# Where the rope scores of a step are issued in a decoder layer: behind product 7 of the step ahead

## The reference

```python
c_q = h @ w_q_down                       # 384 wide, h is the layer norm of x
c_kv = h @ w_kv_down                     # 128 wide, the latent keys and values
q_lat = einsum('bhsd,hdr->bhsr', q_nope(c_q), wuk)           # 32 heads
scores = einsum('bhsr,btr->bhst', q_lat, c_kv)               # latent scores
       + einsum('bhsd,btd->bhst', rope(q_rope(c_q)), k_rope) # rope scores
probs = softmax(mask(scores / sqrt(192)))
out = einsum('bhst,btr->bhsr', probs, c_kv)                  # "values" below
x = x + (out @ wuv per head) @ w_out
```

## Time and profile before

| what | value |
|---|---|
| median of 3 runs | 1907.11 us (1906.49 to 1908.13) |
| profiled execution, its own time | 1908.23 us |
| span in that profile | 1906.4 us |
| PE busy | 1896.1 us, 99% of the span |
| DVE busy | 1548.0 us, 81% |
| ACT busy | 1184.1 us, 62% |
| POOL busy | 1039.9 us, 55% |
| granted TensorE clock | full in every slice |
| chain that ended last | PE 94%, DMA 2%, DVE 2%, POOL 1% |

### The profile page before, as it was taken

One profiled execution on the slowest core, in us unless ns is written; L12 is line 12 of the kernel. 1 busy time (PEld: TensorE's weight loads), 2 busy tenths in 40 slices (PEclk: granted clock), 3 DMA queues, 4 the chain that ended last, 5 costly groups with the idle time before them and its releaser, 6 DMA issues.

```text
span 1906.4 us, 32258 instructions
## 1 busy us (share of the span) xinstructions
PE 1896.1 (99%) x9920; PEld 1595.8 (84%) x9920; DVE 1548.0 (81%) x3168; ACT 1184.1 (62%) x2904; POOL 1039.9 (55%) x1019
## 2 busy tenths in 40 slices
PE   9999999999999999999999999999999999999999
PEld 7888888888888888888888888888888877888887
DVE  6778888888888888888888787887888889996677
ACT  5457767675858575766556555565666668766441
POOL 5458777787869696965555656555665411000000
PEclk9999999999999999999999999999999999999999
DMA  9839575657475665699747375474738386557645
GB/s 362 332 109 318 136 257 136 249 129 260 134 261 145 227 180 192 206 327 314 190 148 230 77 231 149 152 219 124 231 94 276 113 284 233 206 213 258 222 150 176
DMA packets 328154, 393.27 MB, mean 206 GB/s; under 512 B 271616, under 2 KB 272384, under 8 KB 313088
## 3 DMA queue, kind: packets, MB, share of 16 engines
q1 hardware_dynamic: 328064, 392.21, 63.3%
HBM read 236.46 MB, written 155.71 MB: 206 GB/s over the span
## 4 chain that ended last, share of the span: by engine, by line
PE 94%; DMA 2%; DVE 2%; POOL 1%; issue 0%; SPq 0%; ACT 0%; DVEq 0%; POOLq 0%; ACTq 0%
PE at_out L1325 11%; PE at_out L1329 10%; PE at_out L1326 10%; PE at_qbank L55 7%; PE at_qbank L57 7%; PE at_qbank L56 7%; PE at_qbank L1649 3%; PE at_score L1286 3%; PE at_score L1289 2%; PE at_score L1649 2%; PE at_out L1649 2%; PE at_turned L1300 2%; PE at_value L55 2%; PE at_value L56 2%; PE at_value L57 2%; PE at_qbank L1652 2%
## 5 line engine op out<-in xcount | busy, mean ns | idle before, releaser
L2686 DVE TENSOR_TENSOR at_acc<-at_out,at_acc 128x512 f32<-128x512 f32 x640 | 438.5, 688 | 127.6 <-PE at_out L1329 120.4
L2315 POOL TENSOR_TENSOR at_acc<-at_stage,at_acc 128x512 f32<-128x512 f32 x256 | 331.8, 1296 | 174.4 <-ACT at_stage L1791 164.8
L1325 PE MATMUL at_out<-at_wvo,at_val_hi 128*128 128x512 f32 x896 | 365.6, 408 | 2.1 <-DVE at_acc L2686 1.2
L1329 PE MATMUL at_out<-at_wvo,at_val_lo 128*128 128x512 f32 x896 | 351.3, 392 | 0.0
L1326 PE MATMUL at_out<-at_wvo,at_val_hi 128*128 128x512 f32 x896 | 349.9, 391 | 0.0
L1791 ACT ACTIVATE at_stage<-at_out 128x512 f32<-128x512 f32 x256 | 153.0, 599 | 94.1 <-PE at_out L1329 82.0
L1329 PEld LDWEIGHTS at_out<-at_wvo,at_val_lo 128*128 128x128 f32 x896 | 168.1, 188 | 38.8
L1325 PEld LDWEIGHTS at_out<-at_wvo,at_val_hi 128*128 128x128 f32 x896 | 168.7, 188 | 32.6 <-DVE at_acc L2686 6.3
L1326 PEld LDWEIGHTS at_out<-at_wvo,at_val_hi 128*128 128x128 f32 x896 | 169.1, 189 | 25.5
L1832 ACT ACTIVATE at_pT<-at_turned 128x256 fp32r<-128x256 f32 x128 | 49.0, 383 | 227.3 <-PE at_turned L1300 226.4
L1827 ACT ACTIVATE at_probs<-at_probs,at_row_stats 128x128 f32<-128x128 f32 (+1 forms) x512 | 184.1, 361 | 8.9 <-DVE at_row_stats L2633 8.9
(11 more groups left out here) (323 smaller groups left out, 5042.3 us busy)
## 6 DMA issues: line engine op xcount, KB each, us to landing
parts_d<-at_rope_tmp SPq DMA_DIRECT2D x32, 1024.0 KB, 7.1
at_qrope<-parts_d SPq DMA_DIRECT2D x128, 256.0 KB, 4.5
wvo_d<-at_wvo SPq DMA_DIRECT2D x16, 2048.0 KB, 7.6
at_wvo<-wvo_d SPq DMA_DIRECT2D x16, 2048.0 KB, 8.5
ff_w_d<-ff_w SPq DMA_DIRECT2D x21, 1024.0 KB, 6.4
ff_w<-ff_w_d SPq DMA_DIRECT2D x21, 1024.0 KB, 4.8
ab_raw<-in_w_heads SPq DMA_DIRECT2D x32, 576.0 KB, 6.4
wvo_d<-at_wvo SPq DMA_DIRECT2D x16, 1024.0 KB, 9.8
```

The costliest lines, as they stand in the source:

```text
L1325: pe.matmul(out, hi, weight[:, 0], start=start, stop=False, skip_group_check=True)
L1329: pe.matmul(out, lo, weight[:, 0], start=False, stop=True, skip_group_check=True).then_inc(out_ready, 1)
L2315: pool.tensor_tensor(at, stage[group][z][:], at, ALU.add).then_inc(pool_added, 1)
L2686: dve.tensor_tensor(at, outb[FACTORS[name][2]][:], at, ALU.add).then_inc(added, 1)
```

## The change

The four rope-score matmuls of a step leave their place at the head of the step two ahead, and are issued half a step sooner: step s now issues those of step s+3, right behind product 7. Of the first steps, those of step 2 go to the end of `opening`, which is the same place in the order; those of step 4 stay at the head of step 2 of pass 0; step 1 of pass 0 issues none. In the second half of the last pass, where product 7 comes ahead of product 5, they come behind a half of a transposition for cross-attention and ahead of product 5. Nothing is computed otherwise, and no other engine's program changes.

```diff
                 absorb_head(0, first + 8, first + 7)
-
-            def next_scores(m, s, end, kind, first):
+                score_ropes(0, 2, 0)
+
+            def ropes_sooner(m, s, end, kind):
+
+                t = s + 3
+                if t < end and not opens(m, s, 1):
+                    score_ropes(m, t, group_of(kind, t))
+
+            def next_rests(m, s, end, kind, first):
                 use, t = USE[kind], s + 2
-                if t < end:
-                    score_ropes(m, t, group_of(kind, t))
-                if s + 1 < end:
-                    turn(m, s + 1)
                 if t < end:
                     score_rests(m, t, first - AFTER[kind] if t < 4 else first + use[2 * (t // 2) - 3] + 1)
...
-                next_scores(m, s, end, kind, first)
+                if opens(m, s, 2):
+                    score_ropes(m, s + 2, group_of(kind, s + 2))
+                if s + 1 < end:
+                    turn(m, s + 1)
+                next_rests(m, s, end, kind, first)
                 product_1(m, s, kind, first)
...
                     product_7(m, s, kind)
                     cross_turn(s - STEPS // 2, (0,))
+                    ropes_sooner(m, s, end, kind)
                     product_5(m, s, kind)
...
                     product_5(m, s, kind)
                     product_7(m, s, kind)
+                    ropes_sooner(m, s, end, kind)
                     next_latent(m, s, end, kind, first, range(QT - 1, QT))
```

## The result

The change makes the kernel slower by 0.3%: 1912.76 us (1912.19 to 1913.76) against 1906.76 in the same comparison, ratio 1.0031 [1.0023, 1.004], so +6.0 us where +3.4 was forecast. Three kernels made on the way beat both, each clear of the noise: `before_cast`, `short_and_cast` and `mixed`, at the end of the experiments.

What follows compares the result with a forecast made beforehand. PE, busy 1896.1 of 1906.4 us, was taken as the bound. 2.46 + 0.77 + 1.47 - 1.19 - 0.15 = +3.36 us, giving 1911.6 profiled, 1910.5 on the median; own range 1908.9 to 1911.6, stated range 1907.3 to 1914.5.

Steps and rivals of the forecast that it cites:

- Steps 0 to 1: Passes 1 to 6: no room, ACT's queue and the values move by 0.41 us, nothing regained; 6 x 0.41 = +2.46 us.
- a gain beyond the turns: Rival: the wait ahead of the second half of the rope query at step 1 goes too, 0.34 x 7; 1903.4 us; chance 0.03.
- Steps 5 to 6: Passes 0 to 6: room 0.40 us, moved by 0.41, so the values are just missed; 7 x 0.11 = +0.77 us.
- Steps 6 to 7 and the transpositions of step 0: Passes 0 to 6: low parts 0.21 us later, passed through DVE and POOL to PE's transpositions; 7 x 0.21 = +1.47 us.
- late ends cost nothing: Rival: ACT and DVE catch up, only the turns between types are left, -1.34 us; 1905.8 us; chance 0.11.
- more heads run over: Rival: full 0.41 us shift at steps 1 to 2, 4 to 5, 6 to 7; +2.3 and +1.4, 1914.2 us; chance 0.18.
- Absorbed pairs: Steps 2 to 3 and 3 to 4, passes 0 to 6: one turn between fp32 and fp32r gone; 14 x 0.085 = -1.19 us.
- Passes 8 to 14: Heads have only product 4 at the step's end, its addition fits a DVE pause: no change, length kept to 0.1 us.
- a rival at 0.09 a step: The 512-column matmul behind the rope group starts slowly, 0.48 us against 0.40; 0.09 x 124 = +11.2, 1921.7 us; chance 0.06.
- Pass 15, steps 4 on: No term here; pass 15's only term was steps 1 to 3, product 3's wait for DVE partly filled, -0.15 us.
- New waits: Moved rope scores wait for rope queries: nothing waits, 0.7 us to spare at step 5 of pass 7; late query chance 0.02.
- The page's rule on the size of the group: Skill's isolated-matmul formula gives the rope group 0.33 us, not the trace's 0.41; the sum would be some 1.2 us smaller.

Runs made afterwards that it cites:

- before_cast: Kernel before, with ACT's cast of the rope weights behind its copies of the turned probabilities at step 1 of passes 1 to 6; 1903.71 us, ratio 0.9985.
- short_and_cast: Changed kernel with only the two 128-column rope matmuls behind product 7, and ACT's rope-weight cast behind its copies of the turned probabilities; 1902.47 us, ratio 0.9981.
- mixed: Changed kernel with ACT's cast moved; 256-column pair moved in passes 0 to 6, 128-column pair later, nothing at steps 4 to 7 of pass 15; 1900.99 us.
- cast_behind: Changed kernel with ACT's cast of the rope weights behind its copies of the turned probabilities at step 1 of passes 1 to 6; 1909.64 us, ratio 1.0017.
- before_again: The kernel before itself, unchanged, profiled once more to see how one execution differs from the next; 1910.03 us.
- no_rope: Kernel before without the four rope matmuls of a step from step 4 of pass 7 on, all waits kept; executed once, 1886.26 us.

## Why the prediction was right in its size and partly wrong in its steps

The time fell in the stated range, 1907.3 to 1914.5, but above the 1908.9 to 1911.6 of the forecast itself. It is also above the line of 1910.9 from which the prediction called it slower, for which it gave 0.41 against 0.56 for no clear change. And by its own signs the mechanism was incomplete: it was to be wrong "if the later passes change", or if the latent product behind L1279 starts late, and both happened. PE's waits at the late heads grew by 3.8 us (2.6 - 0.4 + 1.6), where 4.5 were forecast.

- *Steps 0 to 1*: +0.41 at the values, as forecast (3.07 for 2.66). But "nothing is regained there" failed. The wait ahead of the second half of the rope query, 0.23 + 0.11 over the usual 0.23 in each of passes 1 to 6, was gone in the changed kernel; step 1 grew by 0.13 only, not 0.41. This was the rival "a gain beyond the turns", given 0.03. Its counter-argument, that the wait is for product 3's addition, which moves by as much as PE does, had the wrong releaser: it is ACT's copy of the latent query, which moves with the values only, while PE comes there later by the rope group too (shown with `cast_behind`). I forecast 2.46 us; 6 x 0.13 = 0.77 came, of which 6 x 0.035 = 0.2 is the price of the place.
- *Steps 5 to 6*, the values just missed: forecast +0.11, measured 10.67 to 10.785, which is 0.08 beside the 0.035 of every step. Right.
- *Steps 6 to 7 and the transpositions of step 0*: forecast +0.21, measured 10.91 to 11.11, +0.20. Right, through the chain of DVE and POOL; 0.15 of it stands at the transpositions, 0.04 at product 5. The rivals "late ends cost nothing" and "more heads run over" are out: in passes 0 to 6 the steps behind 1 to 2 and 4 to 5 grow by no more than the later passes do. Pass 7 has one such late head, at step 5 (+0.15; +0.55 in `cast_behind`).
- *Absorbed pairs*: forecast -1.19, measured +0.01 and +0.03 for steps 2 and 3, so about -0.03 and -0.01 against the other steps, -0.2 in all. The price is no turn between types that the rope group could take away. It moved to where the transpositions take over:

```profile
637.83 1.50 PE L1212 MATMUL at_qbank<-ab_raw 128*128 128x128 f32 x12
639.17 0.49 PE L1300 MATMUL at_turned<-at_ident,at_probs 128*128 128x128 f32 x3
```

  From L1212 to the next start it is 1.34 us. Before, it was 1.25 (634.00 to 635.25), and the rope pair behind it then paid the 0.08. Whoever follows the fp32 pair pays.
- *Passes 8 to 14*: forecast nothing, measured 0.035 in each step, 2.0 us; if it is the same in the other passes, 124 x 0.035 = 4.3 us. This is the term that was missing. I had it as a rival at 0.09 a step and a chance of 0.06, from the distance behind fp32 matmuls. The traces give 0.056 for the long product, 0.026 for the ones behind it, 0.01 in the group itself, and 0.058 that the head gets back. The rival had the direction and the matmul, but 0.09 for the 0.035 of a step: its price was too high for the one matmul, and it had neither the others nor the gain at the head.
- *Pass 15, steps 4 on*: forecast nothing, measured +0.67 at step 4. There the group stands behind a plain fp32 transposition for cross-attention and the values are 0.3 us late. It happens once.
- *New waits* for the rope queries: none, as forecast. No trace shows a new wait ahead of the moved rope matmuls.
- *The page's rule on the size of the group*: the prediction says that with 0.33 us for the group the sum would be some 1.2 us smaller. By its own terms that is 0.5 at step 1 and 0.8 at steps 5 to 6, but also 0.5 at steps 6 to 7, so 1.7. It changes nothing in the forecast, which used 0.41.

From the forecast to what came, term by term: 3.4, +4.3 for the place behind product 7, +1.0 for the absorbed pairs, +0.8 for pass 15, -1.9 at step 1 (0.13 less 0.035, six times, for 2.46), -0.5 at steps 5 to 6 and 6 to 7 (the same 0.035 taken out of what they measured), and -0.3 for steps 5 and 0 of passes 0 to 6 together. Step 5 is shorter by 0.03 there, where every other step is longer, which no run explains. Step 0 is longer by 0.1 in passes 3 and 5, but 0.06 of that also lies between the two executions of the kernel before. The sum is 6.8, against 6.65 by the steps and 6.0 by the time. The range held it because errors of both signs met, which is luck, and 4.3 us of them had no term.

The Trainium skill ("TensorE: Matmul & The Clock Gate", Back-to-back issue gap) gives for a sustained stream some 81 ns a matmul at 128 columns and 131 ns at 512. By the first the trace agrees, 0.17 for two. By the second it does not: 0.22 to 0.24 us in the plain steps of every kernel here, nearer to the formula for an isolated one.

## What to carry to other kernels

When PE is busy 99% of the time, price a moved matmul by the step's whole length with and without it: a rope group of 0.41 us was worth 0.46 in one place and 0.49 in the other, and a pair of 128 columns cost the longer matmul behind it 0.05 to 0.06 us in every order tried here. Before moving PE's work, look at what stands in the helper engines' queues ahead of the one copy that PE waits for; here one cast of 0.83 us, moved behind three copies, gave 2.8 us, as much as the best order of the rope scores gave on top of it (2.7). And check a forecast stretch by stretch against the trace, since a total in range can be two errors of opposite sign.

## What the runs showed of the hardware

After the wait of 1.81 us in pass 15, the granted clock fell to the lower level of 1.2 GHz, and stayed there past 1466 us. The windows of `before_again` (us, length, then the busy time of PE, PEld, DVE, ACT and POOL, the granted clock, DMA share and GB/s):

```profile
1462.00:1464.00 2.00, 1.56 (x6) 1.16 (x7) 1.72 (x4) 0.93 (x2) 1.46 (x3) 1.00 1.02 420
1464.00:1466.00 2.00, 2.00 (x11) 1.95 (x10) 1.73 (x5) 0.30 (x2) 0.76 (x1) 0.51 1.09 388
1466.00:1470.00 4.00, 4.00 (x22) 3.66 (x22) 2.85 (x9) 2.12 (x6) 1.84 (x3) 0.82 0.60 236
```

Step 2 took 10.94 us there in place of 9.69. In the trace, where the same wait was 1.20 us, step 2 took 9.69 and the clock stayed full. Here the late load cost its wait, and then 1.24 us more. In `no_rope` the same wait was 2.94 us, and the granted clock behind it was 0.54 from 1440 to 1442 us and 0.61 to 1444.
